# Cross attention of a two-layer perceiver kernel: the value sums in groups of eight key tiles, and the PSUM buffers dealt out anew

## The chip, the core and the metric

One NeuronCore of a Trainium2 chip runs the whole program. The metric is the device time of one execution in microseconds (us). TensorE is called PE below (its weight loads PEld), VectorE DVE, ScalarE ACT, GpSimd POOL, SyncE SP.

## The reference, cut to what matters

The model has two layers. Each one has a cross attention, a self attention and a feed-forward or mixture-of-experts part. Only the cross attentions are touched. They have B = 2 batches, H = 16 heads of 16 columns, 256 queries and 4096 keys:

```
scores = einsum('bqhd,bkhd->bhqk', q, k) / sqrt(16)      (layer 0; + mask)
scores = einsum('bhqd,bhkd->bhqk', q, k) * 16**-0.5      (layer 1; + (i - j) * w_rel[h])
probs  = softmax(scores, axis=-1)
out    = einsum('bhqk,bkhd->bqhd', probs, v)
```

## The kernel before, in words

`cross_attention` (line 883) runs 32 pairs of head and batch, called heads here and numbered g, and it is called twice, once for each layer: 64 heads in all. Queries and keys are stored as stacks of bf16 pieces, 96 rows for the product and 9 more, among them three rows that take the negated maximum of each query into the product. The work of a head:

- **Pass 1** (`pass1`, line 990): the scores with queries on the partitions, only to find the maximum of each query. There are N1 = 8 steps: 2 query tiles by 4 pieces of 1024 keys, and a step is two matmuls of 512 columns (line 1000) into one of the two halves of `ps1`. DVE takes the maximum of each step (`take_max`, line 1104). Step u waits until the maximum of step u-2, which has the same half, is taken (line 997).
- **The maxima are turned**: DVE reduces the 8 partial maxima and splits the result into three bf16 pieces (`c_rows`, a chain of 5 instructions, lines 1111 and 757 to 760), PE transposes them (`turn_c`, line 1008) into `ps_c`, a part of the bank `ps_m`, and DVE copies them into the query stack (`copy_c`, line 1116), which releases pass 2 of that head.
- **Pass 2** (`pass2`, line 1011): the scores with keys on the partitions, N2 = 16 steps of two key tiles, each step two matmuls of 256 columns (line 1019) into one of the two buffers of `ps2`. ACT takes the exponential (line 1092) into one of 8 slots of `probs` (fp32). Step u waits for the exponential of step u-2 (line 1016).
- **The sums over values** (`pv_group`, line 1023): a group takes GROUP = 2 steps of pass 2, so 4 key tiles, with one fp32 matmul of 256 columns for each (line 1033). The stationary operand has 32 columns, and key tile kt writes partitions 32*(kt%4) to 32*(kt%4)+31 of `ps_o`. So a group is 4 matmuls of the source; each fp32 matmul of the source appears as two instructions, and a group as x8. In the trace these start as two sets of four, the four of a set within 20 ns of each other; such a set is called a quad below.
- **The outputs are turned** (`finish`): ACT copies `ps_o` to `o_sb` (line 1083), PE adds the four partial sums and transposes them by a matmul with `sel4` (line 1044) into `ps_f`, another part of `ps_m`, and DVE divides by the sum of probabilities (lines 1120 and 1122).

The order of PE is written out by hand in `head` (line 1048). While pass 2 of head g runs, pass 1 of head g+1 is spread between its steps at `PASS1_AT` (line 1069), the last group of sums of head g-1 is done at u = 1, its `finish` at u = 5, `turn_c` of head g+1 at u = 15, and steps 0 and 1 of pass 1 of head g+2 at u = 14 and, behind `turn_c`, at u = 15 (line 1064). Every engine works its own list in order; semaphores connect them. DVE's order in a head (line 1125) is maxima 0 to 3 of head g+1, `finish`, maxima 4 to 7, `c_rows`, `copy_c`. ACT's is the 16 exponentials, with the copy of `ps_o` ahead of the third. POOL copies queries and values for later heads, SP loads key stacks four heads ahead.

Of the kernel before, what the change touches and what calls it, by code (L numbers as in the profile page):

```python
# [882 lines left out]
def cross_attention(pr, buffers):  # L883
# [6 lines left out]
    W1 = SK // NC1  # L890
    N1 = QT * NC1
    N2 = KT // 2
    GROUP = 2
    NPV = N2 // GROUP
    SLOTS = 8
    CH = 5
    NK = 16 * len(K_PIECES)
    kst, qall, vall, k_in = buffers.kst, buffers.qall, buffers.vall, buffers.k_in
    with ExitStack() as st:
# [8 lines left out]
        rcp = pr.sb(st, "rcp", [P, QT])  # L908
# [27 lines left out]
        with nc.Block() as block:  # L936
# [50 lines left out]

            @block.tensor
            def _(pe):
                def pass1(g, m, b, u, wait=True):  # L990

                    if u == 0:

                        pe.wait_ge(k_in[m], NK // NBUF * (g - m) + NK + buffers.n_aux)
                        pe.wait_ge(q_ready, g + 1)
                    if wait:
                        pe.wait_ge(mx, N1 * g + u - 1)
                    qt, c = u // NC1, u % NC1
                    for x in range(W1 // 512):
                        mm = pe.matmul(ps1[:, u % 2, x * 512:(x + 1) * 512], qst[:, m, qt * P:(qt + 1) * P],  # L1000
                                       kst[:, m, c * W1 + x * 512:c * W1 + (x + 1) * 512], start=True, stop=True)
                    mm.then_inc(sc1, 1)

# [7 lines left out]
                def pass2(g, m, b, u, wait=True):  # L1011

                    if u == 0:
                        pe.wait_ge(c_ready, g + 1)
                    if wait:
                        pe.wait_ge(probs_ready, N2 * g + u - 1)
                    for x in range(2):
                        kt = 2 * u + x
                        mm = pe.matmul(ps2[:, u % 2, x, :], kst[:, m, kt * P:(kt + 1) * P], qst[:, m, :],  # L1019
                                       start=True, stop=True)  # L1020
                    mm.then_inc(sc2, 1)

                def pv_group(g, b, o, first=False):

                    if o == 0:
                        pe.wait_ge(v_ready, g + 1)
                        if not first:
                            pe.wait_ge(o_copied, g)
                    pe.wait_ge(probs_ready, N2 * g + GROUP * (o + 1))
                    for i in range(2 * GROUP):  # L1030
                        kt = 2 * GROUP * o + i
                        j = kt % 4
                        mm = pe.matmul(ps_o[32 * j:32 * j + 32, b, :], vst[:, b, kt, :],  # L1033
                                       probs[:, (kt // 2) % SLOTS, kt % 2, :],
                                       start=(kt < 4), stop=(kt >= KT - 4), skip_group_check=True)
# [12 lines left out]
                def head(g, h, m, b, place):  # L1048


                    last, first = place == "last", place == "first"
                    for u in range(N2):
                        pass2(g, m, b, u, wait=not (first and u < 2))
                        if u == 1 and not first:
                            pv_group(g - 1, 1 - b, NPV - 1)
                        if u > GROUP and u % GROUP == 1:
                            pv_group(g, b, u // GROUP - 1, first)
                        if u in PASS1_AT and not last:
                            pass1(g + 1, (m + 1) % NBUF, 1 - b, 2 + PASS1_AT.index(u))
                        if u == 5 and not first:  # L1060
                            finish(g - 1, 1 - b, wait=not (isinstance(g, int) and g == 1))
                        if u == N2 - 1 and not last:
                            turn_c(g + 1)
                        if u >= N2 - 2 and not last and place != "last but one":
                            pass1(g + 2, (m + 2) % NBUF, b, u - (N2 - 2))

                PASS1_AT = (1, 3, 5, 7, 8, 10)
                for u in range(N1):  # L1070
                    pass1(0, 0, 0, u, wait=u >= 2)
                for u in range(2):
                    pass1(1, 1, 1, u)
                turn_c(0)
                all_heads(pe, head)
                pv_group(NG - 1, 1, NPV - 1)
                finish(NG - 1, 1)

            @block.scalar
            def _(act):  # L1080
                def copy_o(g, b):
                    act.wait_ge(pv, NPV * (g + 1))
                    nc.scalar.copy(o_sb[:, b, :], ps_o[:, b, :]).then_inc(o_copied, 1)

                def head(g, h, m, b, place):
                    for u in range(N2):
                        if u == 2 and place != "first":
                            copy_o(g - 1, 1 - b)
                        act.wait_ge(sc2, N2 * g + u + 1)
                        if u % GROUP == 0 and not (place == "first" and u < SLOTS):  # L1090
                            act.wait_ge(pv, NPV * g + u // GROUP - SLOTS // GROUP + 1)
                        nc.scalar.activation(probs[:, u % SLOTS, :, :], ps2[:, u % 2, :, :], ACT.Exp).then_inc(  # L1092
                            probs_ready, 1)

                all_heads(act, head)
# [3 lines left out]
            def _(dve):  # L1099
                v = nc.vector  # L1100
                link = Chain(dve, c_chain)
                def take_max(g, b, u):
                    dve.wait_ge(sc1, N1 * g + u + 1)
                    v.tensor_reduce(top[:, b, u // NC1, u % NC1:u % NC1 + 1], ps1[:, u % 2, :], AX, ALU.max).then_inc(  # L1104
                        mx, 1)

                def c_rows(g, b):
# [9 lines left out]

                def finish(g, h, b):
                    dve.wait_ge(o_turned, g + 1)
                    v.reciprocal(rcp[:, :], ps_f[:, :, DH]).then_inc(o_done, 1)  # L1120
                    dve.wait_ge(o_done, 2 * g + 1)
                    v.tensor_tensor(pr.attn[:, :, b, ds(h * DH, DH)], ps_f[:, :, 0:DH], bc(rcp[:, :], 2, DH),
                                    ALU.mult).then_inc(o_done, 1)

                def head(g, h, m, b, place):
# [1391 lines left out]
```

## Time and profile before

| what | value |
|---|---|
| median of 3 runs | 2044.31 us (2043.63 to 2048.55) |
| the profiled execution's own time | 2038.5 us |
| its span | 2036.7 us |
| PE busy | 1728.7 us (85%) |
| DVE busy | 1165.0 us (57%) |
| ACT busy | 842.4 us (41%) |
| cross attention of layer 0, pass 2 | from about 277.5 us to 704 us of the span |
| cross attention of layer 1, pass 2 | from about 1332.4 us to 1758 us of the span |

Times in the profile count from the start of the span. Matmuls are pipelined: a matmul's row lasts from its start to its modelled end, and the next one starts long before that end, so rows of PE overlap and "busy" does not say that the array streams. What an item costs PE is therefore read as the distance from its start to the start of the next item. A row of the timeline merges neighbours of one kind (x8 is eight of them), and the brackets give the idle time of the engine ahead of it and what ended it.

### The profile page before, as it was taken

Reading aid. Unit: us, or ns where it says so; the run is one execution under the profiler, and the core shown is the slowest. Engines: PE = TensorE matmul, PEld = TensorE weight load, DVE = VectorE, ACT = ScalarE, POOL = GpSimd, SP = SyncE. Lnnn points to the kernel's source line nnn. Section 1 sums busy time; section 2 is a strip of 40 time slices with the busy share of each in tenths; the row PEclk is TensorE's granted clock in tenths of the full one; section 3 lists DMA queues with packets and bytes.
Section 4 is the critical chain, followed back from the end, with each engine's and each line's share of the span. In section 5 each row is a group of like instructions: output and inputs, shape, how many; then the busy total and the mean of one; then the engine's idle time right before and its main releaser. Section 6 shows DMA issues by size and latency. Waiting matters only on the chain. (4 is left out here: it accounts for less than half of the span.)

```text
span 2036.7 us, 36753 instructions
## 1 busy us (share of the span) xinstructions
PE 1728.7 (85%) x12160; PEld 963.5 (47%) x12160; DVE 1165.0 (57%) x2107; ACT 842.4 (41%) x1620; POOL 191.4 (9%) x336
## 2 busy tenths in 40 slices
PE   7999979999999836658949998299999999829688
PEld 4444424444444323335828987034444444416587
DVE  5777768888888446436440000388888888336311
ACT  2222236667666602313411111057666667403222
POOL 2222210000000000000121000300000000000000
PEclk9999979999999977879868999589999999869699
DMA  5686584443334152000086998523444333091042
GB/s 190 191 211 203 160 166 63 63 62 57 56 57 62 50 114 24 1 0 1 0 220 223 320 312 293 116 38 58 62 62 62 57 55 44 1 140 39 25 162 73
DMA packets 155759, 208.23 MB, mean 102 GB/s; under 512 B 26628, under 2 KB 128876, under 8 KB 149288
## 3 DMA queue, kind: packets, MB, share of 16 engines
q1 hardware_dynamic: 152076, 203.11, 43.2%
q0 software_dynamic: 1536, 2.17, 0.4%
q10 hardware_dynamic: 2064, 1.87, 0.3%
q8 instruction: 49, 0.80, 0.2%
q14 instruction: 34, 0.28, 0.0%
HBM read 165.50 MB, written 46.26 MB: 104 GB/s over the span
## 5 line engine op out<-in xcount | busy, mean ns | idle before, releaser
L1092 ACT ACTIVATE probs<-ps 128x512 f32<-128x512 f32 x1024 | 573.9, 596 | 287.3 <-PE ps L1019 276.2
L1104 DVE TENSOR_REDUCE top<-ps 128x1 f32<-128x1024 f32 x512 | 601.1, 1219 | 35.4 <-PE ps L1000 33.0
L1000 PE MATMUL ps<-kst,qst 105*128 105x512 bf16 x1024 | 318.7, 394 | 36.2 <-POOL qst L958 28.1
L1019 PE MATMUL ps<-qst,kst 105*128 105x256 bf16 x2048 | 344.5, 276 | 2.3 <-DVE qst L1116 1.8
L1033 PE MATMUL ps_o<-probs,vst 128*32 128x256 f32 x4096 | 328.3, 392 | 0.8 <-ACT probs L1092 0.8
L1019 PEld LDWEIGHTS ps<-qst,kst 105*128 105x128 bf16 x2048 | 176.2, 100 | 215.1 <-ACT probs L1092 62.8
L1000 PEld LDWEIGHTS ps<-kst,qst 105*128 105x128 bf16 x1024 | 65.8, 98 | 189.9 <-DVE top L1104 90.2
L1033 PEld LDWEIGHTS ps_o<-probs,vst 128*32 128x32 f32 x4096 | 80.8, 108 | 109.9 <-issue 88.6
L1921 PE MATMUL ps_h<-xe,wgu 128*128 128x80 f32 x1024 | 126.5, 284 | 1.1 <-ACT xe L1972 0.5
L1921 PEld LDWEIGHTS ps_h<-xe,wgu 128*128 128x128 f32 x1024 | 123.4, 201 | 2.1 <-issue 1.4
L487 PE MATMUL ps_k<-ctxT,wk 128*128 128x512 f32 x256 | 121.4, 597 | 1.5 <-DVE square_weights L652 1.5
L495 PE MATMUL ps_v<-wv,ctxT 128*128 128x512 f32 x256 | 120.3, 592 | 0.0
L964 POOL COPY vst<-vall 128x512 f32 (+1 forms) x64 | 39.1, 613 | 768.2 <-PE ps_o L1033 768.1
L2066 DVE TENSOR_TENSOR hT<-silu,ps_h 128x320 f32<-128x320 f32 x32 | 15.6, 488 | 166.7 <-ACT silu L1978 166.7
L568 ACT COPY vall<-ps_v 128x256 f32 (+1 forms) x64 | 23.8, 372 | 176.8 <-PE ps_v L495 176.8
L743 PE MATMUL ps_t<-consts,xn 128*128 128x128 f32 x56 | 13.8, 428 | 90.7 <-DVE xn L693 52.0
L1265 PE MATMUL ps<-kst,qst 96*128 (+2 forms) x128 | 26.0, 298 | 74.0 <-DMA kst<-k2d 69.3
L651 DVE TENSOR_SCALAR kp<-ps_k,kbias 128x512 bf16<-128x512 f32 x64 | 48.0, 750 | 56.9 <-PE ps_k L487 56.5
L495 PEld LDWEIGHTS ps_v<-wv,ctxT 128*128 128x128 f32 x256 | 48.7, 190 | 61.2 <-issue 61.2
L487 PEld LDWEIGHTS ps_k<-ctxT,wk 128*128 128x128 f32 x256 | 47.9, 192 | 56.4 <-issue 50.3
L604 POOL TENSOR_TENSOR vall<-vall,L_xattn_cv_b 128x256 f32 (+1 forms) x64 | 49.2, 768 | 194.8 <-ACT square_weights L570 194.4
L1116 DVE COPY qst<-ps_m 3x256 bf16<-3x256 bf16 x64 | 18.1, 283 | 86.2 <-PE ps_m L1008 86.2
(323 smaller groups left out, 1910.1 us busy)
## 6 DMA issues: line engine op xcount, KB each, us to landing
kst<-kd SPq DMA_DIRECT2D x384, 128.0 KB
kd<-kp SPq DMA_DIRECT2D x64, 384.0 KB, 2.7
wgu<-in_L_ffn_wg_dram SPq DMA_DIRECT2D x32, 512.0 KB, 4.7
wgu<-in_L_ffn_wu_dram SPq DMA_DIRECT2D x32, 512.0 KB, 5.8
wd<-in_L_ffn_wd_dram SPq DMA_DIRECT2D x32, 512.0 KB, 6.3
w<-in_L_ffn_w_dram SPq DMA_DIRECT2D x16, 1024.0 KB, 5.3
ctx_sb<-in_ctx_dram SPq DMA_DIRECT2D x16, 512.0 KB, 5.8
vd<-square_weights SPq DMA_DIRECT2D x16, 512.0 KB, 4.1
```

The lines of the kernel that those rows point to most:

```text
L487: mm = pe.matmul(ps_k[:, q % 2, :], wk[:, c, q // C, (q % C) * P:(q % C + 1) * P], ctxT[:, par, c, :], start=(c == 0), stop=(c == C - 1))
L495: mm = pe.matmul(ps_v[:, t % 2, :], ctxT[:, par, c, t * P:(t + 1) * P], wv[:, c, :, :].rearrange("p l d -> p (l d)"), start=(c == 0), stop ...
L604: g.tensor_tensor(v, v, pr.row["L0_xattn_cv_b"][:, :], ALU.add).then_inc(v_bias, 1)
L651: link(v.tensor_scalar(kp[:, q, 0, :], ps_k[:, q % 2, :], b, None, ALU.add))
L964: nc.gpsimd.tensor_copy(vst[:, b, :, 0:DH], vall[:, b * KT:(b + 1) * KT, ds(h * DH, DH)]).then_inc(v_ready, 1)
L1000: mm = pe.matmul(ps1[:, u % 2, x * 512:(x + 1) * 512], qst[:, m, qt * P:(qt + 1) * P], kst[:, m, c * W1 + x * 512:c * W1 + (x + 1) * 512], ...
L1019: mm = pe.matmul(ps2[:, u % 2, x, :], kst[:, m, kt * P:(kt + 1) * P], qst[:, m, :], start=True, stop=True)
L1033: mm = pe.matmul(ps_o[32 * j:32 * j + 32, b, :], vst[:, b, kt, :], probs[:, (kt // 2) % SLOTS, kt % 2, :], start=(kt < 4), stop=(kt >= KT ...
L1092: nc.scalar.activation(probs[:, u % SLOTS, :, :], ps2[:, u % 2, :, :], ACT.Exp).then_inc(probs_ready, 1)
L1104: v.tensor_reduce(top[:, b, u // NC1, u % NC1:u % NC1 + 1], ps1[:, u % 2, :], AX, ALU.max).then_inc(mx, 1)
L1265: mm = pe.matmul(ps1[:, j, col:col + keys], stack(qst, pair * 2 + j, b * S + qt * P, P, STK), stack(kst, pair * 2 + j, b * S, keys, STK), ...
L1921: mm = pe.matmul(hview[:, b, i, f, :], wgu[:, b, i, c, f * P:(f + 1) * P], xe[:, b, c, :], start=(c == 0), stop=(c == C - 1))
```

## The change

- GROUP goes from 2 to 4: a head has 4 groups of sums with 16 matmul instructions (four quads) each instead of 8 groups with 8 (two quads). The groups stand at u = 2 (the last one of the head before), 6, 10 and 14.
- `ps2` gets three buffers instead of two, in the order SCORES2; a step waits for the exponential that used its buffer before.
- To make room in PSUM, `ps_o` has one buffer, and `ps_m` is gone: `ps_c` and `ps_f` now lie in half 0 of `ps1`. So pass 1 takes its halves in the order SCORES1 = 1, 0, 1, 0, 1, 1, 0, 1, with `turn_c` ahead of step 1 and `finish` between steps 3 and 6 in half 0.
- Step 5 of pass 1 waits for the maximum of step 4, step 0 for all eight maxima of the head before, and step 6 for the division of `finish`.
- `PASS1_AT` is (0, 2, 4, 6, 8, 9, 10) for steps 1 to 7, and step 0 stands at u = 13. `turn_c` stays at u = 15, with nothing of pass 1 behind it. `finish` moves to u = 7 on PE, behind maximum 4 on DVE, and ACT's copy ahead of exponential 4.

```diff
-    GROUP = 2
+    GROUP = 4
+    SCORES1 = (1, 0, 1, 0, 1, 1, 0, 1)
+    SCORES2 = (0, 1, 2, 0, 1, 2, 0, 1, 2, 0, 1, 2, 0, 1, 2, 1)
+    EARLIER2 = tuple(next(d for d in range(1, N2) if SCORES2[(u - d) % N2] == SCORES2[u]) for u in range(N2))
...
-        ps2 = pr.ps(st, "ps2", [P, 2, 2, S])
-        ps_o = pr.ps(st, "ps_o", [P, B, S])
-        ps_m = pr.ps(st, "ps_m", [P, 512])
-        ps_c = ps_m[0:NPIECE, 0:P].bitcast(BF16)
-        ps_f = ps_m[:, 256:256 + QT * 64].rearrange("p (t d) -> p t d", t=QT)
+        ps2 = pr.ps(st, "ps2", [P, 3, 2, S])
+        ps_o = pr.ps(st, "ps_o", [P, 512])[:, 0:S]
+        ps_c = ps1[0:NPIECE, 0, 0:P].bitcast(BF16)
+        ps_f = ps1[:, 0, 0:QT * 64].rearrange("p (t d) -> p t d", t=QT)
...
-                    if wait:
+                    if u == 5:
+                        pe.wait_ge(mx, N1 * g + u)
+                    elif u == 6 and finished:
+                        pe.wait_ge(o_done, 2 * (g - 1))
+                    elif u == 0 and wait:
+                        pe.wait_ge(mx, N1 * g)
+                    elif u >= 2:
                         pe.wait_ge(mx, N1 * g + u - 1)
...
-                        pe.wait_ge(probs_ready, N2 * g + u - 1)
+                        pe.wait_ge(probs_ready, N2 * g + u - EARLIER2[u] + 1)
...
-                def finish(g, b, wait=True):
+                def finish(g, b, ahead=True):
                     pe.wait_ge(o_copied, g + 1)
-                    if wait:
+                    if ahead:
+                        pe.wait_ge(mx, N1 * (g + 2) + 4)
+                    else:
+                        pe.wait_ge(mx, N1 * NG)
                         pe.wait_ge(o_done, 2 * g)
...
-                        pass2(g, m, b, u, wait=not (first and u < 2))
-                        if u == 1 and not first:
+                        pass2(g, m, b, u, wait=not (first and u < 3))
+                        if u == 2 and not first:
                             pv_group(g - 1, 1 - b, NPV - 1)
-                        if u > GROUP and u % GROUP == 1:
+                        if u > GROUP and u % GROUP == 2:
                             pv_group(g, b, u // GROUP - 1, first)
+                        if u == 7 and not first:
+                            finish(g - 1, 1 - b, ahead=not last)
                         if u in PASS1_AT and not last:
-                            pass1(g + 1, (m + 1) % NBUF, 1 - b, 2 + PASS1_AT.index(u))
-                        if u == 5 and not first:
-                            finish(g - 1, 1 - b, wait=not (isinstance(g, int) and g == 1))
+                            pass1(g + 1, (m + 1) % NBUF, 1 - b, 1 + PASS1_AT.index(u), finished=not first)
                         if u == N2 - 1 and not last:
                             turn_c(g + 1)
-                        if u >= N2 - 2 and not last and place != "last but one":
-                            pass1(g + 2, (m + 2) % NBUF, b, u - (N2 - 2))
-                PASS1_AT = (1, 3, 5, 7, 8, 10)
+                        if u == N2 - 3 and not last and place != "last but one":
+                            pass1(g + 2, (m + 2) % NBUF, b, 0)
+                PASS1_AT = (0, 2, 4, 6, 8, 9, 10)
...
-                        if u == 2 and place != "first":
+                        if u == 4 and place != "first":
                             copy_o(g - 1, 1 - b)
...
-                        if u == 3 and place != "first":
+                        if u == 4 and place != "first":
                             finish(*before)
```

## Rows read from the trace of the kernel before

**Rows 1.** Stretches (start:end, us): busy us of PE, PEld, DVE, ACT, POOL; PEclk, DMA share, GB/s.

```profile
277.50:691.00 413.50, 409.87 (x3642) 175.86 (x3642) 334.50 (x494) 286.20 (x526) 28.01 (x58) 0.99 0.39 62
...
277.51:292.45 14.94, 14.37 (x105) 5.85 (x106) 10.63 (x15) 9.01 (x16) 0.00 (x0) 0.78 0.96 239
```

**Rows 2.** Timeline of DVE (start us, us, line, out<-in): layer 0's last `copy_c`, layer 1's first.

```profile
691.01 0.28 DVE L1116 COPY qst<-ps_m 3x256 bf16<-3x256 bf16 x1 [1.15 <-PE ps_m L1008]
...
1332.39 0.28 DVE L1116 COPY qst<-ps_m 3x256 bf16<-3x256 bf16 x1 [0.54 <-PE ps_m L1008]
```

**Rows 3.** Timeline of PE in one head of layer 0, 505.97 to 519.17 us.

```profile
509.13 0.60 PE L1019 MATMUL ps<-qst,kst 105*128 105x256 bf16 x4
509.66 0.64 PE L1033 MATMUL ps_o<-probs,vst 128*32 128x256 f32 x8
510.23 0.60 PE L1000 MATMUL ps<-kst,qst 105*128 105x512 bf16 x2
510.68 0.56 PE L1044 MATMUL ps_m<-consts,o_sb 128*128 128x64 f32 x4
511.07 0.60 PE L1019 MATMUL ps<-qst,kst 105*128 105x256 bf16 x4
...
513.43 0.38 PE L1019 MATMUL ps<-qst,kst 105*128 105x256 bf16 x2
513.74 0.64 PE L1033 MATMUL ps_o<-probs,vst 128*32 128x256 f32 x8
...
518.44 0.28 PE L1008 MATMUL ps_m<-constsb,cp 128*3 128x128 bf16 x2
518.65 0.61 PE L1000 MATMUL ps<-kst,qst 105*128 105x512 bf16 x2
```

**Rows 4.** PE's sums: timeline cut behind a first quad; the line's durations (ns, min/median/max).

```profile
508.12 0.42 PE L1033 MATMUL ps_o<-probs,vst 128*32 128x256 f32 x4
...
L1033 PE MATMUL ps_o<-probs,vst x4096: 378/402/637, 280.9 to 1756.1; 128*32 128x256 f32 x196
```

**Rows 5.** Timeline of DVE in the same head.

```profile
505.87 4.69 DVE L1104 TENSOR_REDUCE top<-ps 128x1 f32<-128x1024 f32 x4
511.27 0.17 DVE L1120 RECIPROCAL rcp<-ps_m 128x2 f32<-128x2 f32 x1 [0.71 <-PE ps_m L1044]
...
511.70 4.69 DVE L1104 TENSOR_REDUCE top<-ps 128x1 f32<-128x1024 f32 x4
516.43 0.16 DVE L1111 TENSOR_REDUCE cwhole<-top 128x2 f32<-128x8 f32 x1
...
517.23 0.16 DVE L760 TENSOR_TENSOR cp<-crest,cp 128x2 bf16<-128x2 f32 x1
```

**Rows 6.** Start of layer 0's pass 1: PE's first step, DVE's first maximum, PE's third step.

```profile
265.50 1.01 PE L1000 MATMUL ps<-kst,qst 105*128 105x512 bf16 x2 [13.80 <-POOL qst L958]
...
266.55 1.23 DVE L1104 TENSOR_REDUCE top<-ps 128x1 f32<-128x1024 f32 x1 [13.80 <-PE ps L1000]
...
267.84 0.61 PE L1000 MATMUL ps<-kst,qst 105*128 105x512 bf16 x1 [0.47 <-DVE top L1104]
```

**Rows 7.** Timeline of ACT in the head of rows 3.

```profile
506.48 1.09 ACT L1092 ACTIVATE probs<-ps 128x512 f32<-128x512 f32 x2 [0.99 <-PE ps L1019]
507.44 0.38 ACT L1083 COPY o_sb<-ps_o 128x256 f32<-128x256 f32 x1
```

**Rows 8.** Timeline of all engines into the last head of layer 1.

```profile
1744.41 0.27 PE L1008 MATMUL ps_m<-constsb,cp 128*3 128x128 bf16 x2
1744.79 0.28 DVE L1116 COPY qst<-ps_m 3x256 bf16<-3x256 bf16 x1 [1.15 <-PE ps_m L1008]
...
1745.13 0.61 PE L1019 MATMUL ps<-qst,kst 105*128 105x256 bf16 x4 [0.45 <-DVE qst L1116]
1745.56 0.60 ACT L1092 ACTIVATE probs<-ps 128x512 f32<-128x512 f32 x1 [0.87 <-PE ps L1019]
```

**Rows 9.** A stretch of the self attention of layer 0, columns as in rows 1.

```profile
800.67:804.30 3.63, 2.88 (x25) 1.65 (x25) 2.89 (x10) 1.40 (x2) 0.36 (x2) 1.00 0.00 0
```

More of the change, by code:

```diff
@@ L989, in _, with pass1 @@
             def _(pe):
-                def pass1(g, m, b, u, wait=True):
+                def pass1(g, m, b, u, wait=True, finished=True):
                     if u == 0:
@@ L999, in pass1 @@
                     for x in range(W1 // 512):
-                        mm = pe.matmul(ps1[:, u % 2, x * 512:(x + 1) * 512], qst[:, m, qt * P:(qt + 1) * P],
+                        mm = pe.matmul(ps1[:, SCORES1[u], x * 512:(x + 1) * 512], qst[:, m, qt * P:(qt + 1) * P],
                                        kst[:, m, c * W1 + x * 512:c * W1 + (x + 1) * 512], start=True, stop=True)
@@ L1015, in pass2 @@
                     if wait:
-                        pe.wait_ge(probs_ready, N2 * g + u - 1)
+                        pe.wait_ge(probs_ready, N2 * g + u - EARLIER2[u] + 1)
                     for x in range(2):
                         kt = 2 * u + x
-                        mm = pe.matmul(ps2[:, u % 2, x, :], kst[:, m, kt * P:(kt + 1) * P], qst[:, m, :],
+                        mm = pe.matmul(ps2[:, SCORES2[u], x, :], kst[:, m, kt * P:(kt + 1) * P], qst[:, m, :],
                                        start=True, stop=True)
@@ L1032, in pv_group @@
                         j = kt % 4
-                        mm = pe.matmul(ps_o[32 * j:32 * j + 32, b, :], vst[:, b, kt, :],
+                        mm = pe.matmul(ps_o[32 * j:32 * j + 32, :], vst[:, b, kt, :],
                                        probs[:, (kt // 2) % SLOTS, kt % 2, :],
@@ L1076, in _ @@
                 pv_group(NG - 1, 1, NPV - 1)
-                finish(NG - 1, 1)
+                finish(NG - 1, 1, ahead=False)
             @block.scalar
@@ L1082, in copy_o @@
                     act.wait_ge(pv, NPV * (g + 1))
-                    nc.scalar.copy(o_sb[:, b, :], ps_o[:, b, :]).then_inc(o_copied, 1)
+                    nc.scalar.copy(o_sb[:, b, :], ps_o).then_inc(o_copied, 1)
                 def head(g, h, m, b, place):
                     for u in range(N2):
-                        if u == 2 and place != "first":
+                        if u == 4 and place != "first":
                             copy_o(g - 1, 1 - b)
@@ L1091, in head @@
                             act.wait_ge(pv, NPV * g + u // GROUP - SLOTS // GROUP + 1)
-                        nc.scalar.activation(probs[:, u % SLOTS, :, :], ps2[:, u % 2, :, :], ACT.Exp).then_inc(
+                        nc.scalar.activation(probs[:, u % SLOTS, :, :], ps2[:, SCORES2[u], :, :], ACT.Exp).then_inc(
                             probs_ready, 1)
@@ L1103, in take_max @@
                     dve.wait_ge(sc1, N1 * g + u + 1)
-                    v.tensor_reduce(top[:, b, u // NC1, u % NC1:u % NC1 + 1], ps1[:, u % 2, :], AX, ALU.max).then_inc(
+                    v.tensor_reduce(top[:, b, u // NC1, u % NC1:u % NC1 + 1], ps1[:, SCORES1[u], :], AX, ALU.max).then_inc(
                         mx, 1)
@@ L1119, in finish @@
                     dve.wait_ge(o_turned, g + 1)
-                    v.reciprocal(rcp[:, :], ps_f[:, :, DH]).then_inc(o_done, 1)
+                    v.reciprocal(rcp[:, b, :], ps_f[:, :, DH]).then_inc(o_done, 1)
                     dve.wait_ge(o_done, 2 * g + 1)
-                    v.tensor_tensor(pr.attn[:, :, b, ds(h * DH, DH)], ps_f[:, :, 0:DH], bc(rcp[:, :], 2, DH),
+                    v.tensor_tensor(pr.attn[:, :, b, ds(h * DH, DH)], ps_f[:, :, 0:DH], bc(rcp[:, b, :], 2, DH),
                                     ALU.mult).then_inc(o_done, 1)
```

7 lines of the change are left out of this document (3 added, 4 removed).

## The prediction

> **What bounds the kernel now.** I read the clock first, then the period of a head, then PE's and DVE's order inside one. The clock of layer 0's cross attention is 0.99 of full [rows 1], so what PE loses there it loses to waits and not to a slow array. The period comes from DVE's copy of the turned maxima, once per head: 32 copies from 277.51 us, where the second stretch of rows 1 begins, to 691.01 us give (691.01 - 277.51)/31 = 13.34 us, and 32 from 1332.39 to 1744.79 us 13.30 us [rows 2, 8]; mean 13.32. The 64 heads are some 850 of 2036.7 us.
>
> Inside a head the reader should look at PE's distances from start to start [rows 3]. A step of pass 1 takes 0.44 to 0.45 us (510.23 to 510.68), the turn of outputs 0.39 (510.68 to 511.07). Two steps of pass 2 and the entry into a group of sums take 0.53 (509.13 to 509.66), one step with the entry 0.31 (513.43 to 513.74), so a step alone 0.22, and the entry costs 0.31 - 0.22 = 0.09. A group takes 0.57 to the next item (509.66 to 510.23). Its first quad lasts 0.42 and has matmuls of 0.40; the whole lasts 0.64, and the second quad's matmuls are the shortest of the line, 0.38 [rows 4]. So the last one of the first quad starts 0.02 and the last one of the second 0.26 after the group's start: 0.24 per quad. So the exit costs 0.57 - 2 x 0.24 = 0.09, and **each group pays 0.18 us for its two edges**. In all PE needs 16 x 0.22 + 8 x 0.44 + 8 x 0.66 + 0.39 + about 0.1 for the turned maxima (0.21 with the exit from the group before it, 518.44 to 518.65) = 12.8 us, against 13.3 measured. PE's own work is the bound, with half a microsecond of waits.
>
> DVE is close behind. Four maxima take 4.69 us, so with the last one's 1.22 to 1.23 us [rows 6] the pitch is (4.69 - 1.23)/3 = 1.155; `finish` takes 511.70 - 511.27 = 0.43, and the chain of `c_rows` 517.39 - 516.43 = 0.96 [rows 5]. Eight maxima, `finish`, chain and copy are 11.0 us, in which DVE waits for almost nothing but the turned outputs (0.71).
>
> **The change part by part.** *Fewer edges.* Four groups fewer save 4 x 0.18 = 0.72 us a head, if the third and fourth quad cost 0.24 like the second. Such a quad is in no row. The nearest below is 0.22, two pass 2 matmuls with as many columns; the nearest above is 0.33, a quad with the edge behind it, as if every pair paid its edges again. I take 0.24, the same operation one place earlier. The bounds are 8 x 0.02 = 0.2 us less and 8 x 0.09 = 0.7 us more per head. Beside this row, the Trainium skill (TensorE: Matmul & The Clock Gate, "Measured speedup vs the span model") counts for packed tiles only a matmul's length and about 4 ns a tile, with nothing for entering or leaving; by that the merging would save nothing. The trace does not agree, since it shows 0.31 against 0.22 ahead of every group.
>
> *The turned maxima lose their cover.* Before, a step of pass 1 stands between `turn_c` and pass 2, 0.21 us behind the former (518.44, 518.65). Now nothing does. The last head of layer 1 has exactly this order: `turn_c` at 1744.41, copy at 1744.79, pass 2 at 1745.13, 0.72 us [rows 8]. Of that 0.5 is new wait.
>
> *DVE runs dry.* This is the large term. Half 0 is borrowed, so only step 0 of pass 1 is ready when DVE starts the maxima; the rest must come in time, and now groups of 4 x 0.24 + 0.18 = 1.14 us stand ahead of steps 2, 4 and 7. I walk one head from PE's first pass 2 step at 0.00, where DVE begins maximum 0 (some hundredths after its copy). A pass 1 step's data end 0.60 us after its start, DVE starts 0.04 later and PE starts 0.06 after a maximum ends [rows 3, 6].
>
> - PE: pass 2 step 0 at 0.00, pass 1 step 1 at 0.22, pass 2 steps 1 and 2 at 0.66 and 0.88, group at 1.10, pass 1 step 2 at 1.10 + 1.14 = 2.24. DVE would be free at 2.31 after two maxima; the data are there at 2.88: **0.57 idle**.
> - PE: pass 2 steps 3, 4 at 2.68, 2.90, pass 1 step 3 at 3.12, pass 2 steps 5, 6 at 3.56, 3.78, group, pass 1 step 4 at 5.14. DVE is free at 2.88 + 2.31 = 5.19, the data come at 5.78: **0.59 idle**. Maximum 4 ends at 7.01.
> - PE: pass 2 step 7, `finish`, pass 2 step 8; at 6.41 it is at pass 1 step 5. This has the half of step 4 and must wait for maximum 4: 7.07. **PE waits 0.66.**
> - Step 5's data at 7.71, step 6 on PE at 7.73, group at 8.17, step 7 at 9.53 (pass 2 step 10 ahead of it). Maxima 5, 6, 7 begin at 7.71, 8.87 and 10.17, the last ends at 11.39.
> - PE after pass 2 steps 11 to 13 is at step 0 of the next head's pass 1 at 10.63. It has the half of step 7: 11.45. **PE waits 0.82.**
> - Pass 2 step 14 at 11.89, group, step 15 at 13.25, `turn_c` 0.31 later (as from a step into a group), pass 2 of the next head 0.72 after that: **14.28 us**, against 13.32.
>
> Behind these two waits stand all of pass 2 and the sums, since PE works in order; ACT then waits for PE. The chain of `c_rows` ends at 12.4, before `turn_c` at 13.56, so it is not on the path.
>
> *Edits at nothing.* The third buffer of `ps2` gives ACT room it doesn't lack: ACT's pitch is 1.09 - 0.60 = 0.49 us [rows 7], 16 x 0.49 + 0.38 = 8.2 of 14 us. The exponential of step 3 ends at about 2.68 + 0.43 + 0.60 = 3.71 (0.43 from pass 2's start to ACT's, rows 8), just ahead of step 6 at 3.78; if it is late, PE loses some hundredths. ACT's copy (0.38, [rows 7]) ends at about 4.0, ahead of the group at 4.09, the first to write the single `ps_o`; its cover is 0.1 us, and a late copy would move that group. The division ends 0.5 us behind maximum 4, at 7.55, ahead of step 6 at 7.73. SP and POOL load and copy as before, more than a head ahead; nothing of theirs moves.
>
> *Ends.* In each layer 30 periods grow by 0.96: 28.8. The period into the last head has no step 0 to wait for and grows by about 0.1 + 0.5; the last head has fewer edges, -0.5. Before the first head, step 5 waits for maximum 4, once, a lost overlap of about 1.01 + 0.04 + 0.06 = 1.1 us at half clock [rows 6]. Some 29.5 per layer, **59 us in all**: 2038.5 + 59 = 2097.5 against the profiled execution's own time. The median shown is 5.8 us above that time, so 2044.3 + 59 = 2103.
>
> **The rivals.**
>
> *One of the two waits hardly appears*, because DVE is sooner than my walk has it. Without the 0.66 the period is 13.62, +0.30 x 60 = 18: 2062. For it: half a microsecond either way decides. Against: every duration is a row.
>
> *PE becomes dense: faster.* If pass 1's steps 2 and 4 reached DVE before it is free (at 2.31 and 4.6), both PE waits would be gone: 14.28 - 0.66 - 0.82 = 12.80 us, 0.52 less than before; 60 x -0.52 = -31, and the result is 2013. The point is pass 1 step 2: it must start at 1.67 and not at 2.24, so the group at u = 2 would have to take 0.57, the old group's time, and not 1.14. The order in the code speaks against it.
>
> *The edges stay* (the change doesn't do what it says): quads three and four cost 0.33 a pair edge, +0.7 x 62 = 45 us on top, 2147. Against it: the edges are seen at the change from bf16 to fp32 groups, and these become fewer.
>
> *The clock falls.* PE now stands still twice in a head. The first head of layer 0, which begins at the low level of 1.2 GHz and has a mean of 0.78, lasts 14.94 us [rows 1], 1.6 more than the mean; one such loss in four heads is 16 x 1.6 = 26 us more, 2129. Against it: in self attention PE is idle for 3.63 - 2.88 = 0.75 us in 3.63 and is granted 1.00 [rows 9], the level of 2.4 GHz. The Trainium skill (TensorE: Matmul & The Clock Gate, "A second HAM failure mode: psum-queue depth-cycling") says that small idle times between matmul groups, from waiting for PSUM banks, make the clock swing between its levels; that rule would give this case, and rows 9 don't bear it out.
>
> **How the numbers follow.** About 0.3% (6 us) is what a measurement of this kernel can tell. My case 0.68; one wait missing 0.13; dense PE 0.08; edges stay 0.04; clock 0.03; the rest a sum between 2038 and 2050 by cancelling errors, 0.04. Faster 0.08, same 0.04, slower 0.88. The predicted time is 2103. My case's own range is 2103 - 12 (quads at 0.22) to about 2130; taken down to the case with one wait missing, 2055 to 2130 leaves out the dense case and the edges.
>
> **What the profile would show.** The copies of turned maxima 14.2 to 14.3 us apart. DVE's idle time ahead of the maxima, ended by pass 1's matmuls, over 1.1 us in each head, some 70 us. PE's idle time ahead of pass 1, ended by the maxima, 50 to 80 us, in two places of each head: step 5, and step 0 of the next head. PE waiting for DVE's copy in every head, 0.72 us from `turn_c` to pass 2. Groups of 16 that take 1.05 us to the next item. The granted clock still 1.00. A period under 13.3 us, or DVE without idle time ahead of step 2's maximum, would prove me wrong.

## The result and the profile after

The changed kernel takes 2096.85 us (median of 4 runs, 2093.23 to 2100.65), against 2043.97 us for the kernel before in runs on the same chip: a ratio of 1.0259, 95% interval 1.0233 to 1.0284. It is slower by 53 us. The forecast was 2103, range 2055 to 2130.

First the page of the changed kernel: busy time by engine, the granted clock, and the groups of the maxima (L1115, before L1104), pass 1 (L1009, before L1000) and the sums (L1042, before L1033).

```profile
PE 1685.6 (80%) x12160; PEld 1001.9 (48%) x12160; DVE 1171.9 (56%) x2107; ACT 836.8 (40%) x1620; POOL 190.5 (9%) x336
...
PEclk9999979999999966879978998599999999969599
...
L1115 DVE TENSOR_REDUCE top<-ps 128x1 f32<-128x1024 f32 x512 | 609.1, 1220 | 119.2 <-PE ps L1009 111.3
L1009 PE MATMUL ps<-kst,qst 105*128 105x512 bf16 x1024 | 317.5, 394 | 107.8 <-DVE top L1115 79.7
...
L1042 PE MATMUL ps_o<-probs,vst 128*32 128x256 f32 x4096 | 274.3, 385 | 1.4 <-ACT probs L1103 1.4
```

PE's busy time fell from 1728.7 to 1685.6 us, all of it and more in the group of the sums, and the kernel became slower. In the kernel before, DVE's idle time ahead of the maxima that pass 1 ended was 33.0 us, and PE's ahead of pass 1 that the maxima ended 5.5 us. Now they are 111.3 and 79.7: each engine waits for the other. Part of DVE's number has nothing to do with the change: 27.5 us before and 25.1 now lie ahead of the first maximum of the two layers. Of the rest, 64.6 us are ahead of maxima 2 and 4 and 19.8 ahead of maximum 5. Of PE's 79.7, 77.5 are ahead of steps 0 and 5.

DVE's timeline of the changed kernel: first and last copy of the turned maxima in layer 0, which answer to [rows 2], and the middle of one head, which answers to [rows 5].

```profile
278.44 0.28 DVE L1127 COPY qst<-ps 3x256 bf16<-3x256 bf16 x1 [0.58 <-PE ps L1017]
...
717.15 0.28 DVE L1127 COPY qst<-ps 3x256 bf16<-3x256 bf16 x1 [0.67 <-PE ps L1017]
...
506.87 2.36 DVE L1115 TENSOR_REDUCE top<-ps 128x1 f32<-128x1024 f32 x2 [0.23 <-issue]
509.61 2.35 DVE L1115 TENSOR_REDUCE top<-ps 128x1 f32<-128x1024 f32 x2 [0.38 <-PE ps L1009]
512.45 1.22 DVE L1115 TENSOR_REDUCE top<-ps 128x1 f32<-128x1024 f32 x1 [0.49 <-PE ps L1009]
...
514.38 3.63 DVE L1115 TENSOR_REDUCE top<-ps 128x1 f32<-128x1024 f32 x3
```

The period is (717.15 - 278.44)/31 = 14.15 us, and 14.13 in layer 1, against a mean of 13.32 before. Four maxima in a row of 4.69 us [rows 5] have become 2 + 2 + 1, with idle time ahead of maxima 2 and 4. The stretch that answers to the first of [rows 1], in the same columns:

```profile
278.36:717.06 438.70, 388.39 (x3636) 192.53 (x3636) 337.45 (x494) 283.13 (x526) 28.00 (x58) 0.99 0.37 58
```

The clock is 0.99 as before, while PE is now busy for 388.39 of 438.70 us, where it was for 409.87 of 413.50.

PE's timeline in the same head, which answers to [rows 3]: the group behind pass 2 step 2, the wait ahead of pass 1 step 5, the wait ahead of step 0 of the next head, and the stretch from `turn_c` to the next head.

```profile
507.43 0.60 PE L1028 MATMUL ps<-qst,kst 105*128 105x256 bf16 x4
507.96 1.07 PE L1042 MATMUL ps_o<-probs,vst 128*32 128x256 f32 x16
508.96 0.61 PE L1009 MATMUL ps<-kst,qst 105*128 105x512 bf16 x2
...
512.86 0.38 PE L1028 MATMUL ps<-qst,kst 105*128 105x256 bf16 x2
513.73 0.61 PE L1009 MATMUL ps<-kst,qst 105*128 105x512 bf16 x2 [0.49 <-DVE top L1115]
...
516.58 0.82 PE L1028 MATMUL ps<-qst,kst 105*128 105x256 bf16 x6
518.07 0.60 PE L1009 MATMUL ps<-kst,qst 105*128 105x512 bf16 x2 [0.67 <-DVE top L1115]
...
520.15 0.27 PE L1017 MATMUL ps<-constsb,cp 128*3 128x128 bf16 x2
520.87 0.39 PE L1028 MATMUL ps<-qst,kst 105*128 105x256 bf16 x2 [0.45 <-ACT probs L1103]
```

From pass 2 step 8 to pass 1 step 5 it takes 513.73 - 512.86 = 0.87 us, of which step 8 is 0.22: 0.65 us of wait. From step 11 to pass 1 step 0 it takes 518.07 - 516.58 = 1.49, three steps being 0.66: 0.83 of wait. From `turn_c` to pass 2 it takes 0.72. The last row teaches something: the profile puts the wait down to ACT, because pass 2 step 0 waits for an exponential and for DVE's copy, and DVE's copy (520.46 to 520.74 in this trace) is what ended it; the exponential that step 0 needs is that of step 12 of the head before, done some 2.8 us earlier. The one that happened to end at 520.85 is step 15's. Copy and pass 2 stand at the same distances behind `turn_c` in short_groups and turn_earlier, where no exponential ends there.

The rest of the program has not changed. Of the 58.8 us between the two spans, the two stretches between first and last copy hold 25.2 and 25.8; about 6 us lie between the two cross attentions, in code that is the same. That stretch took 638 to 653 us in the profiles of this study, so these 6 us are within its own variation. Another 0.8 lie behind the last copy. The 51 us of the two stretches and the 0.9 by which the first copy of layer 0 comes later (278.44 against 277.51) are the effect, and they agree with the medians' 53.

### The profile page after: what moved, and what is told of

Its sections match the earlier page's. It is cut to its first block and busy times, and to the rows that moved or that the text cites. A ratio compares the mean times of both kernels' runs of the same rounds, so it can differ in the third digit from the quotient of the medians.

```text
span 2095.5 us, 36503 instructions
## 1 busy us (share of the span) xinstructions
PE 1685.6 (80%) x12160; PEld 1001.9 (48%) x12160; DVE 1171.9 (56%) x2107; ACT 836.8 (40%) x1620; POOL 190.5 (9%) x336
## 5 line engine op out<-in xcount | busy, mean ns | idle before, releaser
L1115 DVE TENSOR_REDUCE top<-ps 128x1 f32<-128x1024 f32 x512 | 609.1, 1220 | 119.2 <-PE ps L1009 111.3
L1009 PE MATMUL ps<-kst,qst 105*128 105x512 bf16 x1024 | 317.5, 394 | 107.8 <-DVE top L1115 79.7
L1028 PEld LDWEIGHTS ps<-qst,kst 105*128 105x128 bf16 x2048 | 186.3, 100 | 204.4 <-ACT probs L1103 63.8
L1042 PE MATMUL ps_o<-probs,vst 128*32 128x256 f32 x4096 | 274.3, 385 | 1.4 <-ACT probs L1103 1.4
L1009 PEld LDWEIGHTS ps<-kst,qst 105*128 105x128 bf16 x1024 | 75.3, 99 | 236.9 <-issue 123.6
L1042 PEld LDWEIGHTS ps_o<-probs,vst 128*32 128x32 f32 x4096 | 106.9, 109 | 99.8 <-issue 31.0
L1127 DVE COPY qst<-ps 3x256 bf16<-3x256 bf16 x64 | 18.2, 284 | 90.9 <-PE ps L1017 90.9
```

The lines of the kernel that those rows point to most:

```text
L1009: mm = pe.matmul(ps1[:, SCORES1[u], x * 512:(x + 1) * 512], qst[:, m, qt * P:(qt + 1) * P], kst[:, m, c * W1 + x * 512:c * W1 + (x + 1) * ...
L1028: mm = pe.matmul(ps2[:, SCORES2[u], x, :], kst[:, m, kt * P:(kt + 1) * P], qst[:, m, :], start=True, stop=True)
L1042: mm = pe.matmul(ps_o[32 * j:32 * j + 32, :], vst[:, b, kt, :], probs[:, (kt // 2) % SLOTS, kt % 2, :], start=(kt < 4), stop=(kt >= KT - 4 ...
```

## The experiments

Each run was timed against the kernel before on the same chip. "Period" is the mean distance of the copies of the turned maxima in layer 0 and layer 1.

**Groups of four alone.** The kernel before with one number changed.

```diff
-    GROUP = 2
+    GROUP = 4
```

> Kernel before with GROUP = 4 alone (groups at u = 1 of the next head, 5, 9, 13; all buffers and the order of pass 1 as before). Theory A (the loss of the change comes from the order and the shared halves, the longer groups by themselves gain): PE saves 4 x 0.18 us of edges per head; a walk with the rows of before gives DVE idle ahead of maxima 3 and 4, because the group at u = 5 delays pass 1 step 4 and finish, and a period of about 12.85 us against 13.32: 62 x -0.47 = -29, so 2015 us, range 2000 to 2035. Rival B (long groups are what holds DVE up, whatever the buffers): period 13.6 or more, 2060 or more.

Measured: 2099.52 us, ratio 1.0261 (1.0226 to 1.0296), periods 14.18 and 14.12. Rival B's number was right and my walk was wrong, but B's reason, DVE whatever the buffers, is only half of it. PE's timeline of this kernel, one head, with pass 1 as L1000 and pass 2 as L1019:

```profile
512.39 0.39 PE L1019 MATMUL ps<-qst,kst 105*128 105x256 bf16 x2
513.39 0.61 PE L1000 MATMUL ps<-kst,qst 105*128 105x512 bf16 x2 [0.61 <-DVE top L1104]
...
515.81 0.81 PE L1019 MATMUL ps<-qst,kst 105*128 105x256 bf16 x4
516.88 0.39 PE L1019 MATMUL ps<-qst,kst 105*128 105x256 bf16 x2 [0.26 <-ACT probs L1092]
```

The first two rows are B's half: 513.39 - 512.39 - 0.22 = 0.78 us in which step 6 of pass 1 waits for a maximum. The last two are ACT's. With two score buffers PE can run only two steps ahead of ACT. A long group lets ACT run out of scores, and after it the four steps that lie between groups go at ACT's pace: from 515.81 to 516.88, 1.07 us for two steps that need 0.44. PE's weight loads of pass 2 waited 220.0 us for ACT here, against 62.8 in the kernel before. Summed over this head, PE's distances hold about 1.2 us of waits for ACT and 0.8 for DVE. I had walked only a part of the head with ACT in it. This split is read from the trace; no run has the old order with long groups and a third buffer. So longer groups by themselves lose, with the old buffers, in the old order.

**Two score buffers in the changed kernel.**

```diff
-    SCORES2 = (0, 1, 2, 0, 1, 2, 0, 1, 2, 0, 1, 2, 0, 1, 2, 1)
+    SCORES2 = (0, 1) * 8
...
-                        pass2(g, m, b, u, wait=not (first and u < 3))
+                        pass2(g, m, b, u, wait=not (first and u < 2))
```

> Changed kernel with two of the three score buffers of pass 2 in use (order 0, 1, 0, 1), each step waiting for the exponential of step u-2; nothing else. The prediction called the third buffer room that ACT does not lack; by that, no change: 2097 us. Against it a walk with the rows of the changed kernel: step 2 would wait for exponential 0 (0.25 us), step 6 for exponential 4, which stands behind ACT's copy of the outputs (0.75 us), both ahead of pass 1 step 4 on PE: period about 15.1, 60 x 1.0, about 2158 us.

Measured: 2165.22 us, ratio 1.0586 (1.0552 to 1.0619), periods 15.17 and 15.16. The walk held (15.1). PE's timeline of this kernel, steps 5 and 6 of pass 2 and the group behind them:

```profile
526.83 0.39 PE L1028 MATMUL ps<-qst,kst 105*128 105x256 bf16 x2
527.59 0.39 PE L1028 MATMUL ps<-qst,kst 105*128 105x256 bf16 x2 [0.37 <-ACT probs L1103]
527.91 1.07 PE L1042 MATMUL ps_o<-probs,vst 128*32 128x256 f32 x16
```

Step 6 comes 0.76 us after step 5 instead of 0.22. The third buffer is worth 1.0 us a head here, 68 us in all. The prediction had called it room that ACT doesn't lack. With it, PE's weight loads of pass 2 waited 63.8 us for ACT, and 210.0 without it.

**Steps 2 and 4 of pass 1 ahead of the groups.**

```diff
+                        if u in (2, 6) and not last:
+                            pass1(g + 1, (m + 1) % NBUF, 1 - b, 1 + PASS1_AT.index(u), finished=not first)
                         if u == 2 and not first:
                             pv_group(g - 1, 1 - b, NPV - 1)
...
-                        if u in PASS1_AT and not last:
+                        if u in PASS1_AT and u not in (2, 6) and not last:
```

> Changed kernel, with steps 2 and 4 of pass 1 moved ahead of the group of sums at u = 2 and u = 6 instead of behind it; nothing else. Theory A (DVE runs dry because a group stands ahead of these steps): DVE's idle time ahead of maximum 2 goes (0.5 to 0), that ahead of maximum 4 too (one of 0.45 may come ahead of maximum 3), PE's wait at step 5 goes, the one at step 0 of the next head stays near 0.8 since DVE's chain is then the bound: period 13.65 to 13.75 against 14.10, 60 x -0.4 = -24, so about 2073 us. Rival C (PE waits for maxima because each half is used twice in a row, at steps 4 and 5 and at 7 and 0, whenever DVE starts): the waits stay as they are, period 14.1, 2097 us.

Measured: 2060.12 us, ratio 1.0079 (1.0054 to 1.0104), periods 13.64 and 13.59. The page's groups of this kernel and the place of step 0 in PE's timeline:

```profile
L1117 DVE TENSOR_REDUCE top<-ps 128x1 f32<-128x1024 f32 x512 | 603.8, 1220 | 72.2 <-PE ps L1009 59.4
...
521.80 0.82 PE L1028 MATMUL ps<-qst,kst 105*128 105x256 bf16 x6
523.28 0.61 PE L1009 MATMUL ps<-kst,qst 105*128 105x512 bf16 x2 [0.66 <-DVE top L1117]
```

DVE's idle time ahead of the maxima falls from 111.3 to 59.4 us. Ahead of maxima 2 and 4 it is gone (64.6 us in all before this move, 1.3 now), but 25.5 have come ahead of maximum 3, as the expectation allowed, and the start of the two layers has its 25 as before. In the same head PE's step 5 follows step 8 without a wait (518.74 to 518.96), while the wait at step 0 is as large as before (523.28 - 521.80 - 0.66 = 0.82). Over all heads PE's wait at step 5 falls from 33.7 to 2.6 us, and the one at step 0 stays at 43.7. That is theory A and not rival C: the halves are used as before, and only the work ahead of two steps was moved. It gains 0.5 us a head where 0.4 was expected.

**`turn_c` ahead of pass 2 step 15.**

```diff
                     for u in range(N2):
+                        if u == N2 - 1 and not last:
+                            turn_c(g + 1)
                         pass2(g, m, b, u, wait=not (first and u < 3))
...
-                        if u == N2 - 1 and not last:
-                            turn_c(g + 1)
```

> Changed kernel, with turn_c ahead of pass 2 step 15 instead of behind it (the chain of maxima ended about 1 us before, so it need not wait). Theory A (0.73 us from turn_c to pass 2 are uncovered): step 15 and its entry cost, about 0.3 us, fall into that time: period 13.8, 62 x -0.3 = -19, about 2078 us. If the time behind turn_c were hidden anyway (by DVE being the bound), the period would stay 14.1 and the time 2097.

Measured: 2065.31 us, ratio 1.0107 (1.0075 to 1.0140), periods 13.69 and 13.68. PE's timeline of this kernel: `turn_c`, then steps 15 and 0 in one row, then pass 1.

```profile
512.20 0.28 PE L1017 MATMUL ps<-constsb,cp 128*3 128x128 bf16 x2
512.41 0.91 PE L1028 MATMUL ps<-qst,kst 105*128 105x256 bf16 x4
513.16 0.59 PE L1009 MATMUL ps<-kst,qst 105*128 105x512 bf16 x2
```

The whole step of 0.22 us and the exit and entry around it fall into the 0.72 us of the copy: 0.45 us a head, where 0.3 was expected. The uncovered turn was on the path.

**Step 0 of the next head behind the last group.**

```diff
-                        if u == N2 - 3 and not last and place != "last but one":
+                        if u == N2 - 2 and not last and place != "last but one":
```

> Changed kernel, with step 0 of the next head's pass 1 behind the group of sums at u = 14 instead of at u = 13; nothing else. In the changed kernel PE waits 0.83 us there, with pass 2 step 14 and the group behind it. Theory A (the wait blocks work that needs nothing from DVE): step 14 and the group (1.3 us) fill the wait, the maximum is taken by the time PE comes to step 0, the chain of maxima ends about when turn_c is reached: period 13.1 to 13.3 against 14.10, 60 x -0.9 = -54, about 2045 us. Rival D (DVE's own chain is the bound, so that the wait moves to turn_c): period 13.9 or more, 2085 or more.

Measured: 2069.42 us, ratio 1.0138 (1.0099 to 1.0176), periods 13.71 and 13.70: half of what theory A wanted, and rival D is out as well. PE's timeline of this kernel, steps 11 to 13, step 14, the group, and step 0:

```profile
523.23 0.82 PE L1028 MATMUL ps<-qst,kst 105*128 105x256 bf16 x6
524.30 0.39 PE L1028 MATMUL ps<-qst,kst 105*128 105x256 bf16 x2 [0.25 <-ACT probs L1103]
524.62 1.07 PE L1042 MATMUL ps_o<-probs,vst 128*32 128x256 f32 x16
525.62 0.60 PE L1009 MATMUL ps<-kst,qst 105*128 105x512 bf16 x2
```

The wait for DVE at step 0 is gone (525.62 - 524.62 = 1.00, the group alone), and none has come at `turn_c`. But now four steps of pass 2 follow each other, and the fourth must wait for the exponential three steps back: 1.07 us from step 11 to step 14 where 0.66 would do, 0.41 of new wait. The wait for DVE had covered one for ACT.

**Groups of two in the changed kernel.**

```diff
-    GROUP = 4
+    GROUP = 2
...
-                        if u > GROUP and u % GROUP == 2:
-                            pv_group(g, b, u // GROUP - 1, first)
+                        if u >= 4 and u % 2 == 0 or u == N2 - 1:
+                            pv_group(g, b, u // 2 - 2 if u < N2 - 1 else 6, first)
...
-                        if u == 4 and place != "first":
+                        if u == 3 and place != "first":
                             copy_o(g - 1, 1 - b)
```

> Changed kernel with GROUP = 2 again (groups at u = 2, 4, 6, 8, 10, 12, 14, 15; ACT's copy ahead of exponential 3), buffers and order of pass 1 as in the changed kernel. It separates the group's length from the shared halves. Theory A: eight groups pay 4 x 0.18 more in edges, but less work stands ahead of steps 2, 4 and 7, so the waits at step 5 and step 0 shrink from 0.65 and 0.83 to about 0.1 and 0.5; period about 13.9, 60 x -0.2 = -12, about 2085 us. If the group's length made no difference to DVE, the edges would come on top: 14.8, 2140.

Measured: 2075.93 us, ratio 1.0174 (1.0140 to 1.0208), periods 13.85 and 13.87, as theory A had it (13.9). In this order the edges that the change saves are less than what the longer groups cost by starving DVE. PE's wait at step 5 is gone in this trace, and the one at step 0 is 0.45 (512.78 - 512.11 - 0.22):

```profile
512.11 0.39 PE L1028 MATMUL ps<-qst,kst 105*128 105x256 bf16 x2
512.78 0.60 PE L1009 MATMUL ps<-kst,qst 105*128 105x512 bf16 x2 [0.28 <-DVE top L1115]
```

The run says one thing more. With short groups the change still costs 0.54 us a head (13.86 against 13.32), some 32 of the 53 us. So more than half of the loss comes with the new buffers and order even at the old group length: the 0.45 us at step 0, and the 0.72 us behind `turn_c`, for the most part. The longer groups add 0.28.

**Three moves together**, steps 2 and 4 ahead of their groups, `turn_c` ahead of step 15, step 0 at u = 14: the three diffs above.

> Changed kernel with three moves together: steps 2 and 4 ahead of their groups, turn_c ahead of pass 2 step 15, step 0 behind the group at u = 14. Theory A: waits left on PE are about 0.1 at step 2, 0.3 from turn_c to pass 2 and some tenths at turn_c for the chain; period 12.7 to 12.9, 60 x -1.3 = -78, about 2020 us, faster than the kernel before. If the gains of the moves overlap (all three shorten the same chain), period 13.2, 2045.

Measured: 2023.81 us, ratio 0.9915 (0.9889 to 0.9941), periods 13.00 and 12.96. With the change's own buffers and groups, in another order, the kernel is 0.85% faster than the one before. Alone the moves gained 0.5, 0.45 and 0.45 us a head, together 1.15, so some of it overlaps.

**A new order, first try.** Step 3 behind the group at u = 2, `finish` behind the group at u = 6, and behind the one at u = 14 `turn_c`, then step 0, then step 15.

```diff
+                        if u in (0, 2, 6, 8, 9):
+                            step({0: 1, 2: 2, 6: 4, 8: 5, 9: 6}[u])
                         if u == 2 and not first:
                             pv_group(g - 1, 1 - b, NPV - 1)
                         if u > GROUP and u % GROUP == 2:
                             pv_group(g, b, u // GROUP - 1, first)
+                        if u == 2:
+                            step(3)
+                        if u == 10:
+                            step(7)
+                        if u == 6 and not first:
+                            finish(g - 1, 1 - b, ahead=not last)
+                        if u == N2 - 2 and not last:
+                            turn_c(g + 1)
+                        if u == N2 - 2 and not last and place != "last but one":
+                            pass1(g + 2, (m + 2) % NBUF, b, 0)
```

> Changed kernel with its buffers and groups but another order on PE: pass 1 steps 2 and 4 ahead of the groups at u = 2 and 6, step 3 right behind the former, finish right behind the latter, and behind the group at u = 14 first turn_c, then step 0 of the next head's pass 1, then pass 2 step 15, so that turn_c's copy is covered by 0.65 us of work. Theory A: PE is then bound by its own work, 16 x 0.22 + 8 x 0.44 + 4 x 1.10 + 0.39 + 0.1 = 11.9, with 0.3 to 0.6 of waits left (the chain of maxima ahead of turn_c): period 12.2 to 12.5 against 14.10, 60 x -1.75 = -105, about 1992 us. If DVE's chain (11.0 us of work a head and its latencies) ends later than PE's work, 12.8 and 2015.

Measured: 2043.62 us, ratio 0.9999 (0.9982 to 1.0015), periods 13.26 and 13.25, a miss by 50 us, and worse than the three moves. DVE's timeline of this kernel in one head:

```profile
510.01 1.22 DVE L1120 TENSOR_REDUCE top<-ps 128x1 f32<-128x1024 f32 x1 [0.51 <-PE ps L1009]
511.60 0.17 DVE L1136 RECIPROCAL rcp<-ps 128x2 f32<-128x2 f32 x1 [0.36 <-PE ps L1056]
...
512.47 3.63 DVE L1120 TENSOR_REDUCE top<-ps 128x1 f32<-128x1024 f32 x3 [0.36 <-PE ps L1009]
```

Step 3 right behind the group feeds DVE but leaves ACT without scores for another 0.44 us; pass 2 step 6 then waits 0.4 us for ACT, step 4 of pass 1 behind it comes late, and DVE is idle 0.51, 0.36 and 0.36 us. I had walked DVE and PE and not ACT.

**Two more orders.** The first puts steps 3, 5, 6, 7 at u = 3, 7, 8, 11, on top of the three moves.

```diff
+                        step({0: 1, 2: 2, 3: 3, 6: 4}, u)
                         if u == 2 and not first:
                             pv_group(g - 1, 1 - b, NPV - 1)
...
+                        step({7: 5, 8: 6, 11: 7}, u)
```

> Kernel three_moves with pass 1 step 3 at u = 3 instead of 4, step 5 at u = 7 behind finish instead of 8, step 6 at u = 8, step 7 at u = 11 instead of 10. In three_moves pass 2 step 14 waits 0.42 us for exponential 11, since steps 11, 12, 13 follow each other behind a pass 1 step, and DVE has 0.4 us idle ahead of maximum 3. Theory A (waits of PE on ACT and on DVE are what is left, not work): the wait at step 14 goes, turn_c waits 0.2 for the chain: period 12.6 against 12.90, 60 x -0.3 = -18, about 2006 us. If nothing changes (2024), what is left at step 14 was hidden by the chain anyway.

Measured: 2019.64 us, ratio 0.9887 (0.9868 to 0.9907), periods 12.89 and 12.86: a gain of 0.1 us a head over the three moves, where 0.3 was expected. The medians alone don't tell the two kernels apart, since their intervals overlap; the periods do. In its trace the wait of 0.42 us at step 14 is gone and `turn_c` waits 0.20 for the chain, both as expected. The rest is a wait that wasn't: 0.11 us ahead of step 6 of pass 1, which comes 0.33 behind pass 2's step 8 instead of 0.22. The second order moves a group too:

```diff
+                        step({0: 1, 2: 2, 3: 3, 6: 4, 11: 7}, u)
                         if u == 2 and not first:
                             pv_group(g - 1, 1 - b, NPV - 1)
-                        if u > GROUP and u % GROUP == 2:
-                            pv_group(g, b, u // GROUP - 1, first)
+                        if u in (6, 11, 14):
+                            pv_group(g, b, (6, 11, 14).index(u), first)
...
+                        step({7: 5, 8: 6}, u)
+                        if u == N2 - 2 and not last:
+                            turn_c(g + 1)
+                        if u == N2 - 2 and not last and place != "last but one":
+                            pass1(g + 2, (m + 2) % NBUF, b, 0)
```

> As order_a, but the group at u = 10 goes to u = 11 behind step 7, and at u = 14 behind the group come turn_c, then step 0 of the next head's pass 1, so that step 15 and step 0 cover the 0.73 us from turn_c to pass 2. Theory A (dense PE, by the items' distances of the changed kernel): 12.0 us of work and 0.2 to 0.4 of waits, period 12.2 to 12.5, 60 x -0.5 against three_moves, about 1990 us. If step 7 ahead of the group must wait for maximum 5 by more than 0.3, or ACT waits take over, 12.7 and 2012.

Measured: **1991.35 us, ratio 0.9760 (0.9741 to 0.9778)**, periods 12.43 and 12.40, 50 us faster than the kernel before. Its stretch of one head (columns as in rows 1), PE's group at u = 14 with `turn_c` and step 0, and the end of DVE's chain with the copy:

```profile
490.40:502.70 12.30, 12.26 (x119) 6.08 (x120) 10.70 (x16) 8.74 (x18) 0.96 (x2) 1.00 0.44 64
...
501.51 1.07 PE L1042 MATMUL ps_o<-probs,vst 128*32 128x256 f32 x16
502.47 0.27 PE L1017 MATMUL ps<-constsb,cp 128*3 128x128 bf16 x2
502.68 0.60 PE L1009 MATMUL ps<-kst,qst 105*128 105x512 bf16 x2
...
502.25 0.16 DVE L760 TENSOR_TENSOR cp<-crest,cp 128x2 bf16<-128x2 f32 x1
502.78 0.28 DVE L1128 COPY qst<-ps 3x256 bf16<-3x256 bf16 x1 [0.37 <-PE ps L1017]
```

The chain of the maxima ends at 502.41, just ahead of `turn_c`, and step 0 of pass 1 stands in the time of the copy. PE is busy for 12.26 of 12.30 us, with the same matmuls as in the changed kernel, whose head of 14.10 us has 12.49 of busy time. Whether this order would do as much with the old groups of two was not run. PE's own work was worked out as 12.8 us a head with them, which is more than this whole period, so at least some 0.4 us of the gain needs the longer groups, by that estimate.

## Why the prediction was right

- *PE's own work and the edges.* Right in kind. The term was mis-sized: a group of 16 takes 508.96 - 507.96 = 1.00 us to the next item, where 4 x 0.24 + 0.09 = 1.05 was taken. The whole lasts 1.07 and its last matmul 0.38, so that one starts 0.69 after the first; less the spread of 0.02 inside a quad and the 0.24 from the first quad to the second, the two further distances are 0.43 together, 0.215 each. So a part of the 0.24 is paid once per group and is one more edge. Four groups at 0.05 less are 0.2 us a head: that is within 0.02 the difference between the forecast period, 14.28, and the 14.10 us from pass 2 step 0 at 506.77 to the next head's at 520.87.
- *The uncovered turn.* 0.72 us as in [rows 8]; turn_earlier shows that it was on the path.
- *A misreading of before.* DVE was said to wait for almost nothing but the turned outputs (0.71 us). In the head of [rows 5] it also stood idle for 1.36 us ahead of its copy, until `turn_c`. The walk doesn't use the sentence.
- *DVE runs dry.* Idle ahead of maxima 2 and 4 as walked: 0.57 and 0.59 forecast, 0.38 and 0.49 in the brackets of the trace. The shorter group is 0.05 of each difference, and some 0.05 are a matter of counting, since a maximum of 1.22 us lets the next begin after 1.155. Ahead of maximum 2 there are another 0.10, because DVE began maximum 0 at 506.87 and not with pass 2 at 506.77. steps_first shows the cause: with these two steps ahead of the groups the idle time at these two places is gone. "Some 70 us" was too little for the page's 111.3: at the two places it is 64.6, but the sum left out the 25 us at the start of the two layers and a third place, 19.8 us ahead of maximum 5, which the walk has (0.27, from 7.44 to 7.71). And the term was called the large one without a split; short_groups shows that at the old group length DVE still stands idle 0.15 to 0.32 us ahead of each of the maxima 2 to 5.
- *PE's two waits.* 0.66 and 0.82 forecast, 0.65 and 0.83 measured, at steps 5 and 0. The forecast of 50 to 80 us of PE idle time ahead of pass 1 came out at 79.7.
- *The third buffer.* This step failed: "The third buffer of `ps2` gives ACT room it doesn't lack", because ACT's sum, 8.2 of 14 us, is far from full. two_buffers was 68 us slower than the changed kernel, and group_only, with two buffers, 53 slower than the kernel before, where 29 faster had been expected. ACT is busy for 9.15 of the 14.10 us and still sets the pace right behind a long group, if there are only two buffers. The failure didn't touch the time forecast, since the change has the third buffer, but leaving ACT out of the walk did spoil the expectations for group_only, step0_later and new_order.
- *Ends.* Forecast 29.5 us a layer, though its terms add up to 30.0 (28.8 + 0.6 - 0.5 + 1.1); measured 25.2 and 25.8 between the copies and 0.9 ahead of the first. The total of 59 is closer to the medians' 53 than the terms deserve: the quads' 0.18 us, 60 times, are 11 too many, so the others must have been some 4 too few. Which ones wasn't found, and that the two errors cancel in part is luck. That the profiled execution's own time, 2097.38 us, meets the forecast 2097.5 is luck: it contains the 6 us between the layers.
- *Rivals.* The clock didn't fall. PE's clock was 0.99 over layer 0's stretch with two waits of 0.65 and 0.83 and one of 0.5 us in each 14.1 us, as rows 9 had it and against the passage of the Trainium skill (TensorE: Matmul & The Clock Gate, "A second HAM failure mode: psum-queue depth-cycling") that the prediction weighed. The edges didn't stay (1.00 us for a group of 16 against two times 0.57). Dense PE (which was worked out as 12.80 us a head) is what order_b reaches and passes, but by another order of work.

What remains open: how the 1.15 us of the three moves divide where they overlap, and what order_b still loses. In the head shown it takes 502.68 - 490.34 = 12.34 us from one step 0 of pass 1 to the next, and its timeline has four short waits of PE in it (0.20 ahead of pass 2 step 1, 0.11 and 0.05 ahead of pass 1 steps 6 and 7, 0.07 at `turn_c`), which leaves 11.9 of work; none of the four was taken away alone. Open too: how the 0.54 us that short_groups still loses divide between the borrowed half, the single `ps_o` and the order, and what the last order would do with groups of two.

## What to carry to other kernels

When a buffer is borrowed or a unit of work made longer on an in-order engine, walk one period with every engine that it feeds, and ask what each has ready when the long item begins: here a group of 1.0 us ahead of a step of 0.4 starved DVE twice a head, and it came back to PE as a wait of 0.65 us at step 5 and of 0.83 at step 0, where a half is used twice in a row. A saving in busy time (43 us on PE) says nothing until such waits are counted. Here the cure wasn't to undo the change but to order it: feed the slow reader before the long group, put independent work behind an operation whose result has to travel through two engines, and walk ACT too, even where it is busy for only two thirds of the period.

## What the runs showed of the hardware

- Going from bf16 matmuls with 128 columns of weights to the fp32 ones with 32 and back has a price at each change, 0.09 us at the entry (0.31 against 0.22) and some 0.1 at the exit. I had not expected that the first pitch inside a group is part of it: starts of neighbouring quads are 0.24 us apart once and then 0.215. The Trainium skill's model of packed tiles (TensorE: Matmul & The Clock Gate, "Measured speedup vs the span model") has neither.
- Where a matmul waits for two semaphores, the profile can name the wrong one: for pass 2 step 0 of the changed kernel it named ACT in 48 of the 64 heads ("0.45 <-ACT probs") and DVE's copy in 16, and in short_groups the copy in all 64, for the same 0.72 or 0.73 us behind `turn_c`. The timeline of the other engines decides such a case. In PE's timeline of short_groups:

```profile
514.88 0.28 PE L1017 MATMUL ps<-constsb,cp 128*3 128x128 bf16 x2
515.61 0.39 PE L1028 MATMUL ps<-qst,kst 105*128 105x256 bf16 x2 [0.45 <-DVE qst L1127]
```
